# Whole fp32 operands in the attention products, one head to each half of the array, in place of rounded pairs with zero blocks

## The reference, cut to what matters

```python
q = split_heads(layernorm(x) @ Wq) * DH ** -0.5         # 32 x 16 x 256 x 64
k, v = split(context @ Wkv)                             # 77 rows each
k = concatenate((null_k, k)); v = concatenate((null_v, v))   # 78 rows
attn = softmax(q @ k.T)                                 # 256 x 78 per head
out = layernorm((attn @ v) @ Wout)
x = x + tanh(g_xattn) * out
x = x + tanh(g_ffn) * experts(layernorm(x))             # 32 experts, 8 per token
```

## Time and profile before

| | |
|---|---|
| median of three runs | 2156.69 us |
| the profiled execution, its span | 2156.4 us |
| TensorE busy | 2034.8 us (94%) |
| VectorE busy | 1768.4 us (82%) |
| ScalarE busy | 1387.1 us (64%) |
| GpSimd busy | 1204.5 us (56%) |
| mean granted TensorE clock | 0.974 |

### The profile page before, as it was taken

The page is one execution under the profiler, slowest core; times in us unless marked ns, Lnnn a source line. Parts: engine busy times, 40 slices in busy tenths (PEclk is TensorE's granted clock), DMA queues, the critical chain, the costliest instruction groups (busy, mean ns, idle before and its releaser), DMA issues. The chain is left out here.

```text
span 2156.4 us, 43812 instructions
## 1 busy us (share of the span) xinstructions
PE 2034.8 (94%) x14306; PEld 1884.7 (87%) x14306; DVE 1768.4 (82%) x4190; ACT 1387.1 (64%) x4030; POOL 1204.5 (56%) x1324
## 2 busy tenths in 40 slices
PE   7999689999999999999997889999999999999995
PEld 7888589999999999999997778988988888888884
DVE  4544258899999999999997766668999999999996
ACT  3322357677777777777774347777777777777771
POOL 0000202777777777777777600006777777777775
PEclk9999889999999999999998899999999999999997
DMA  9876489988888888788886999999999999999997
GB/s 275 280 242 216 140 240 297 304 262 249 246 252 252 252 249 250 248 249 246 248 259 224 298 360 286 287 285 365 403 403 402 397 397 395 391 392 399 393 366 280
DMA packets 442777, 645.86 MB, mean 300 GB/s; under 512 B 204984, under 2 KB 317337, under 8 KB 440089
## 3 DMA queue, kind: packets, MB, share of 16 engines
q1 hardware_dynamic: 393400, 508.79, 71.0%
q0 software_dynamic: 49152, 134.28, 17.2%
HBM read 325.18 MB, written 317.72 MB: 298 GB/s over the span
## 5 line engine op out<-in xcount | busy, mean ns | idle before, releaser
L1710 POOL DMA_INDIRECT parts<-results_dram,kept_index x512 | 516.1, 1008 | 382.7 <-DMA results_dram<-y 219.0
L848 POOL DMA_INDIRECT pages_dram<-rows,kept_index x512 | 509.4, 995 | 167.0 <-issue 139.1
L927 ACT ACTIVATE exps<-sim,minus_max 128x78 f32<-128x78 f32 x1024 | 320.8, 365 | 50.5 <-DVE minus_max L1028 49.9
L927 ACT ACTIVATION_READ_ACCUMULATOR exps<-sim,minus_max 128x1 f32 x1024 | 252.3, 247 | 0.0
L1731 ACT ACTIVATE w_h<-w_raw 128x768 fp32r<-128x768 f32 x159 | 134.0, 843 | 149.7 <-DMA w_raw<-in_experts 149.7
L1819 DVE SCALAR_TENSOR_TENSOR parts<-parts,kept_weight 128x256 f32<-128x256 f32 x448 | 213.6, 477 | 1.8 <-DMA parts<-dense_dram 0.7
L1916 PE MATMUL xps<-ident,xin 128*128 128x128 f32 x1272 | 167.0, 275 | 18.1 <-DVE wq_l L1781 7.9
L1793 DVE TENSOR_TENSOR w_l<-w_raw,w_h 128x768 fp32r<-128x768 f32 x159 | 151.7, 954 | 38.6 <-ACT w_h L1731 38.4
L140 PE MATMUL yps<-w_h,hid_h 128*128 128x256 f32 x636 | 180.0, 283 | 0.7 <-DVE hid_l L1876 0.7
L142 PE MATMUL yps<-w_l,hid_h 128*128 128x256 f32 x636 | 178.7, 281 | 0.0
L141 PE MATMUL yps<-w_h,hid_l 128*128 128x256 f32 x636 | 178.2, 280 | 0.0
(11 more groups left out here) (270 smaller groups left out, 7206.5 us busy)
## 6 DMA issues: line engine op xcount, KB each, us to landing
xin<-pages_dram SPq DMA_DIRECT2D x159, 512.0 KB, 10.5
results_dram<-y SPq DMA_DIRECT2D x159, 512.0 KB, 9.6
w_raw<-in_experts SPq DMA_DIRECT2D x159, 385.0 KB, 9.5
pages_dram<-blank SPq DMA_DIRECT2D x108, 512.0 KB, 4.0
pages_dram<-blank SPq DMA_DIRECT2D x12, 1536.0 KB, 8.2
values_dram<-values SPq DMA_DIRECT2D x16, 1024.0 KB
v_main<-values_dram SPq DMA_DIRECT2D x64, 256.0 KB
keys_h_dram<-keys_h SPq DMA_DIRECT2D x16, 616.0 KB, 4.8
```

Of the source, the lines that this page charges most:

```text
L848: pool.indirect_dma_start(dram["pages"], bass.IndirectOffsetOnAxis(ap=kept_index[:, at:at + 1].bitcast(U32), axis=0), buffer(batch)[:, k / ...
L927: last = act.activation(exps[u % 2][:, h, :], scores(u)[:, h // 4, h % 4, :], ACT.Exp, bias=minus_max[u][:, h:h + 1], accum_out=row_sum[u] ...
L1710: pool.indirect_dma_start(parts[slot(batch, t)][:, k, :], None, done, bass.IndirectOffsetOnAxis(ap=kept_index[:, at:at + 1].bitcast(U32), ...
```

## The change

Queries, transposed weights, keys and values of the attention stage are kept as one fp32 tile each, and their products are plain fp32 matmuls.

- Scores: each head has a product of its own. Its 64 rows of `qT` and `kT` lie in the upper or the lower 64 rows of the array, the two heads of a pair alternate, and the two write different banks of `sim`. A unit has eight products of 78 columns in place of twelve of 156.
- Values: `v` is 78 rows by 16 heads by 64 columns. Each head's product writes the upper or the lower 64 partitions of the output. A step PV has four products of 256 columns in place of twelve.
- Transposes: each head's 78 weights are one transpose, so each unit has two steps of four (T0a and T0b, and so on): 32 a batch in place of 20.
- Evictions: Q and T are copied once, on ScalarE; there is no low tile. X, N2 and PV keep theirs (`SPLIT`). `RING` and `BANK` are written anew to fit.
- `normalise` has one product over 78 columns in place of two.
- The context stage writes keys and values once, by VectorE, and stores half the bytes. A batch loads its keys with one DMA and its values with one.
- At the start of the attention stage the zeroing and the placing of null rows in `v_rest` are gone.

The products for X, Q, O, L, R and the whole expert stage stay.

```diff
-RING = ["X", "N2", "Oa", "T0a", "Ob", "T1a", "L", "Q0", "T1b", "Q1", "PV0a", "PV0b", "T2a", "R", "T3a", "Q2", "T3b", "Q3",
-        "PV1a", "PV1b"]
+RING = ["X", "N2", "Oa", "T0a", "T0b", "Ob", "T1a", "T1b", "L", "Q0", "Q1", "PV0a", "PV0b", "T2a", "T2b", "R", "T3a", "T3b", "Q2",
+        "Q3", "PV1a", "PV1b"]
+SPLIT = [n for n in EVICTED if n in ("X", "N2") or n[0] == "P"]
...
-    kT = [sb(f"kT_{s}", [P, PAIRS, 2 * J], F32R) for s in "hl"]
-    v_main = [sb(f"v_main{i}", [P, 2, PAIRS, P], F32R) for i in range(2)]
-    v_rest = [sb(f"v_rest{i}", [P, 2, 2, HP, P], F32R) for i in range(2)]
-    qT = [sb(f"qT_{s}", [P, PAIRS, N], F32R) for s in "hl"]
+    kT = sb("kT", [P, PAIRS, J])
+    v = [sb(f"v{i}", [J, HEADS, DH]) for i in range(2)]
+    qT = sb("qT", [P, PAIRS, N])
...
-            pe.wait_ge(ring_lo, nth(EVICTED, "Q3", b - 1))
-            pe.wait_ge(keys_loaded, 64 * (b + 1))
+            pe.wait_ge(ring_hi, nth(EVICTED, "Q3", b - 1))
+            pe.wait_ge(keys_loaded, 16 * (b + 1))
...
             for i in range(HP):
                 pair = half * HP + i
-                last = split_product(pe, sim[u % 2][:, i // 2, (i % 2) * 2 * J:(i % 2 + 1) * 2 * J],
-                                     [t[:, pair, tt * P:(tt + 1) * P] for t in qT], [t[:, pair, :] for t in kT])
+                for parity, rows_of in enumerate(halves):
+                    last = pe.matmul(sim[u % 2][:, parity, i * J:(i + 1) * J], qT[rows_of, pair, tt * P:(tt + 1) * P],
+                                     kT[rows_of, pair, :], start=True, stop=True)
...
-                u = int(name[1])
+                u, first = int(name[1]), HP * "ab".index(name[2])
                 pe.wait_ge(probs_ready, UNITS * b + u + 1)
                 for i in range(HP):
-                    last = pe.transpose(ps[:, i * P:(i + 1) * P], probs[u % 2][:, i * P:(i + 1) * P], ident[:, :])
+                    last = pe.transpose(ps[0:J, i * P:(i + 1) * P], probs[u % 2][:, first + i, :], ident[:, :])
...
-                for i, pair in enumerate(pairs):
-                    split_product(pe, ps[:, i * N:(i + 1) * N], [main_values(b, part, HP * half + pair) for part in range(2)],
-                                  [t[:, pair, :] for t in pT], start=i == 0, stop=False)
-                pe.wait_ge(ring_lo, nth(EVICTED, f"T{2 * half + 1}b", b))
-                for i, pair in enumerate(pairs):
-                    last = split_product(pe, ps[:, i * N:(i + 1) * N], [rest_values(b, part, half, pair) for part in range(2)],
-                                         [t[0:PAIRS * REST, HP, :] for t in pT], start=False, stop=i == 1)
+                pe.wait_ge(ring_hi, nth(EVICTED, f"T{2 * half + 1}b", b))
+                first = HP * "ab".index(name[3])
+                for i in range(2):
+                    for rows_of in halves:
+                        head = first + 2 * i + (rows_of.start > 0)
+                        last = pe.matmul(ps[rows_of, i * N:(i + 1) * N], v[par][:, PAIRS * half + head, :], pT[:, head, :], start=True, stop=True)
...
         def low(name, b):
-            if not runs(name, b):
+            if name not in SPLIT or not runs(name, b):
                 return skip()
```

More of the change, by code:

```diff
@@ L223, in staged @@
         return s.rearrange("p (c n) -> p c n", c=shape[1]) if len(shape) == 3 else s
[L225 removed]
+    keys_out = dram["keys"].rearrange("b p f -> p b f")
     def size(t):
@@ L363, in step @@
                         continue
[L364 to L378, removed]
+                    skip()
             step(-1)
@@ L428, in step @@
                         continue
+                    dve.wait_ge(full, at(PRODUCTS, name, g))
                     ps = bank(name)
                     if name[0] == "K":
-                        high, low = (tile[:, :, int(name[2]) % KPART, :] for tile in keys[key_unit(name, g) % KSLOTS])
-                        last = dve.tensor_tensor(low, ps[:, 0:CCOLS].rearrange("p (b m) -> p b m", m=M), high.bitcast(F32),
-                                                 ALU.subtract)
-                    else:
-                        t, half = int(name[1]), int(name[2])
-                        high, low = (values[value_unit(name, g) % VSLOTS][0:size(t), part, half * 512:(half + 1) * 512] for part in range(2))
-                        last = dve.tensor_tensor(low, ps[0:size(t), :], high.bitcast(F32), ALU.subtract)
+                        pair, unit = int(name[2]), key_unit(name, g)
+                        if pair % KPART == 0 and unit >= KSLOTS:
+                            dve.wait_ge(keys_stored[unit % KSLOTS], 16 * (unit // KSLOTS))
+                        last = dve.tensor_copy(keys[unit % KSLOTS][:, :, pair % KPART, :], ps[:, 0:CCOLS].rearrange("p (b m) -> p b m", m=M))
+                    else:
+                        t, half, unit = int(name[1]), int(name[2]), value_unit(name, g)
+                        if half == 0 and unit >= VSLOTS:
+                            dve.wait_ge(values_stored[unit % VSLOTS], 16 * (unit // VSLOTS))
+                        last = dve.tensor_copy(values[unit % VSLOTS][0:size(t), half * 512:(half + 1) * 512], ps[0:size(t), :])
                     signal(last)
@@ L622, in attention_phase @@
     weight_tiles = dram["weights"].rearrange("(b t p) e -> b p t e", t=TT, p=P)
[L624 to L634, removed]
+    halves = [slice(0, DH), slice(DH, P)]
     def buffer(batch):
@@ L670, in load_keys @@
         def load_keys(batch):
[L671 to L674, removed]
+            sp.dma_start(kT[:, :, 0:M], dram["keys"][batch].rearrange("p (q m) -> p q m", m=M)).then_inc(keys_loaded, 16)
         def load_values(batch):
[L678 to L689, removed]
+            sp.dma_start(v[batch % 2][0:M, :, :].rearrange("m h d -> m (h d)"),
+                         dram["values"][batch * M:(batch + 1) * M, :]).then_inc(values_loaded[batch % 2], 16)
         def fill_pages(b, i):
@@ L702, in fill_pages @@
                          blank[:, :, :].unsqueeze(1).broadcast_to([P, pages, PQ, D])).then_inc(filled[i], 16)
-        sp.dma_start(null_v[:, :], dram["null_kv"][1:2, :]).then_inc(null_loaded, 16)
+        for values in v:
+            sp.dma_start(values[M:J, :, :], dram["null_kv"][1:2, :].unsqueeze(1).broadcast_to([1, HEADS, DH])).then_inc(null_v_loaded, 16)
         with nc.allow_non_contiguous_dma(reason="one column of 64 elements"):
-            for half, _ in halves:
+            for half in halves:
                 sp.dma_start(null_k[half, :], dram["null_kv"][0:1, :].rearrange("a d -> d a")).then_inc(null_k_loaded, 16)
@@ L805, in gpsimd @@
         pool.wait_ge(made, 3)
-        for part in kT:
-            for (half, _), (_, col) in zip(halves, reversed(halves)):
-                last = pool.memset(part[half, :, col:col + J].bitcast(F32), 0.0)
-        last.then_inc(keys_zeroed, 1)
-        pool.wait_ge(keys_zeroed, 1)
         def prepare():
-            for t in (*(v[:, :, :, :].rearrange("p s q d -> p (s q d)") for v in v_main),
-                      *(v[:, :, :, :, :].rearrange("p s f q d -> p (s f q d)") for v in v_rest)):
-                last = pool.memset(t.bitcast(F32), 0.0)
-            last.then_inc(zeroed, 1)
             pool.memset(blank[:, :, :], 0.0).then_inc(blank_made, 1)
@@ L967, in step @@
             if b == -2:
-                act.wait_ge(null_loaded, 16)
-                act.activation(null_rows[:, 0, :, :], null_v[:, :].unsqueeze(1).broadcast_to([1, 2, DH]), ACT.Copy).then_inc(null_hi, 1)
                 act.wait_ge(null_k_loaded, 32)
-                for (half, col), null in zip(halves, null_keys()):
-                    last = act.activation(kT[0][half, :, col + M], null, ACT.Copy)
-                last.then_inc(null_k_hi, 1)
+                act.activation(kT[:, :, M], null_k[:, 0:1].broadcast_to([P, PAIRS]), ACT.Copy).then_inc(null_k_set, 1)
             if b == 0:
@@ L991, in step @@
                     exp(2, b)
-                if name == "T0a" and here:
+                if name == "T0b" and here:
                     exp(3, b, 0, PAIRS // 2)
-                if name == "T1a" and here:
+                if name == "T1b" and here:
                     exp(3, b, PAIRS // 2, PAIRS)
@@ L1317, in free @@
                     else:
-                        pe.wait_ge(ring_lo, nth(EVICTED, held, at))
+                        pe.wait_ge(ring_lo if held in SPLIT else ring_hi, nth(EVICTED, held, at))
                     return
```

98 lines of the change are left out of this document (31 added, 67 removed).

## The result

The changed kernel takes 2166.03 us (median of four runs, 2164.46 to 2170.26), the kernel before beside it 2155.63 (2154.43 to 2160.22). The ratio is 1.0045, with a 95% interval of 1.003 to 1.0061. The forecast was 2282 us, so of 126 us that were to be lost, 10 were. The profiled execution took 2167.09 us for a span of 2165.0, so some 2 us lie outside the span, and not the 0.3 us that were taken for it ahead of the prediction.

A forecast was written before the change was run, and what follows sets the result against it. TensorE was taken to bound the kernel. Transposes 0.92, scores 1.12, values 1.51 and hand-overs 0.40 make 3.95 us a batch, times 32 is 126, less 1: 2156.4 + 126 - 1 = 2282 us; 8-in-10 range 2090 to 2340.

The forecast's parts named there:

- If the two halves of the array take turns: Attention stage, TensorE: products on different array halves do not overlap; 3.95 us more a batch, 2282 us; chance 0.45.
- the case side by side: Attention stage: score and value products on different array halves run together; GpSimd's 25.5 us a batch bounds, 2095 us; chance 0.21.
- The argument against it: Against array halves overlapping: no row shows two products overlap but for the pipeline's tail; no start under 0.11 us after another.
- The prices of a whole product: TensorE, attention stage: 0.20 us per whole fp32 score product, 32 a batch; 0.46 per value product, 16 a batch.
- Transposes and hand-overs: TensorE, per batch: eight transpose steps of 0.37 us, 2.96 in all; five net switches between product kinds at 0.08, 0.40.
- TensorE's list of the side-by-side rival: TensorE's work per batch if both product kinds overlap across array halves: 24.5 us, under GpSimd's 25.5; chance 0.21.
- next to nothing: TensorE's waits in the attention stage of the kernel before: the longest is 0.4 us in 680 us.
- ScalarE's evictions: Named danger: TensorE might wait for ScalarE's copies of Q and T, which now alone free their banks; forecast then wrong.
- About 1 us is saved once: Start of the attention loop: the first score no longer waits for Q3's low tile; about 1 us saved once.
- VectorE and ScalarE: Attention stage, per batch: VectorE near 20 us, ScalarE's list 22.3 us, both covered by TensorE.
- The sign: Whole kernel: slower, chance 0.69; faster 0.24; within 0.3% 0.07.
- The mixed rival: Attention stage: only one product kind overlaps across array halves; 2164 us if values do, 2179 if scores do; chance 0.24.

The follow-up runs named there:

- the run without the wait: Changed kernel with VectorE writing X's low tile before the second normalisation and the last maximum of a batch; 2099.84 us, ratio 0.974 to the kernel before.

## Why the prediction was wrong

- **"If the two halves of the array take turns"** is the step that failed. It carried 0.45 of the chance and 7 of the 31.4 us; the case side by side, with 0.21, was the right one. The Trainium skill, "TensorEngine Tiling (Array Packing)", section "Key Properties", says that tiles of the array load and multiply independently, in parallel; the trace agrees (pairs 7 ns apart). The argument against it, that no start comes less than 0.11 us after the one before, came from products that leave no half of the array free, which cannot show it. Nor does it hold for all of them: behind the block of transposes at 811.17 the last one starts at 811.51 and the next product at 811.54.
- **The prices of a whole product were right**: 0.20 forecast for a score and 0.22 to 0.23 measured in one half alone; 0.46 for a value product and 0.43 to 0.45 measured. Only the division by two was missing. The 0.20 was a little low because the pace of the transposes was read too short: their starts are 0.109 us apart, and 0.37 for a step of four holds only three such distances, since the next product follows the last transpose at once.
- **Transposes and hand-overs**: 2.96 + 0.40 forecast. The eight steps take 0.41, 0.40, 0.79, 1.08 and 0.83 us, in all 3.51 (the first two in the windows above, the rest in windows like them), and the hand-overs lie in these and in the blocks.
- **TensorE's list of the side-by-side rival**: 24.5 us forecast, 25.8 measured, of which the two blocks of scores are 0.8 more.
- **The missed wait.** That TensorE waits for "next to nothing" was read from the kernel before and kept for the new order. No step of the prediction walked `RING` with the new `BANK`: who held the bank of each step, and where that holder's last reader stands on its own engine. What it named as a danger was ScalarE's evictions; it was VectorE's, on a tile that the change leaves alone. It cost 2.1 us a batch and the clock.
- **"About 1 us is saved once"** at the start of the loop: 27.7 us were. The batches up to 390 us were taken to be like that of the earlier trace rows, which is a later one. What was placed at the start did delay a product: the null rows stood ahead of the second batch's keys in SyncE's list, and TensorE waited 7.08 us for these keys; how long it would have waited without the null rows, no run shows.
- **VectorE and ScalarE** came out as forecast: 20.4 us for "near 20", 22.0 for 22.3. The context stage stayed at 60 of 60 us.
- **The sign** was right, but for another reason. The rival's 2095 us is close to the 2099.84 of the run without the wait, partly by chance: its batch is 1 us longer than that rival's, and the start gave more. The mixed rival's 2164 us is nearest to the 2166 measured, by luck alone: both kinds overlap, and a wait that no rival had makes up the difference.

## What to carry to other kernels

A trace without an operation of the new kind gives its price in the old arrangement, and the arrangement has to be priced apart: put one product of the new kind in one half alone beside the alternating pair. After any change to an order of steps or to buffers, walk each step to the last reader of what lay in its bank before, and look at what stands ahead of that reader on its engine. A short list with one wait of 2 us in each round can cost more than the list saved, since the clock can fall too.

## What was not expected of the hardware

- Passes in different halves start 7 ns apart, and TensorE found such pairs where they stood up to four passes apart in the program.
- A whole fp32 product of 256 columns takes 0.43 us in a row of them, whether it fills 64 or 128 columns, 78 or 128 rows, and shows as two records. One of 78 columns on 64 rows takes 0.22, two passes of 0.112, each as long as a rounded product of 156 columns.
- A block of values in halves costs some 0.23 us at its ends: its first pair starts 208 ns behind the product before it and is followed after 260, and the next step starts 310 behind its last pass. Over the full width, where no halves are used, these are 120, 219 and 216.
- With a wait of 2.1 to 2.5 us in each batch, the granted clock fell to its lower level in about every second batch; with 0.44 us in each it stayed at 1.00. A wait is not all that it falls for: with the scores in one half the waits were 1.0 us each, and the clock from 600 to 800 was 0.89. What made it fall there is open.
